# Moving the ternary weight rounding of a gated attention and feed-forward block from VectorE to GpSimd, with its readers moved to later steps

## The reference

```python
def weight_quant(w):
    scale = 1.0 / jnp.clip(jnp.mean(jnp.abs(w)), 1e-05)
    return jnp.clip(jnp.round(w * scale), -1, 1) / scale
...
h = bit_linear(x, w1)                       # 256 -> 1024, activations rounded to 8 bits, w1 ternary
h = depthwise_conv1d(h.transpose(0, 2, 1), conv_w, conv_b)
h = jax.nn.silu(h.transpose(0, 2, 1))
return bit_linear(h, w2)                    # 1024 -> 256, the same way
...
x = x + jnp.tanh(g_xattn[0]) * attention(_layernorm(x), ctx_1024, ctx_1024, Wq, Wk, Wv, Wo)   # 16 heads of 16
x = x + jnp.tanh(g_ffn[0]) * ffn(_layernorm(x), w1, conv_w, conv_b, w2)
```

## Time and profile before

| | us |
|---|---|
| median of 3 runs | 236.0 |
| lowest and highest | 234.7, 236.79 |
| span of the profiled execution | 235.2 |
| TensorE busy in it | 215.8 |
| VectorE busy | 190.4 |
| ScalarE busy | 161.9 |
| GpSimd busy | 122.2 |

### The profile page before, as it was taken

The page is one execution under the profiler, slowest core; times in us unless marked ns, Lnnn a source line. Parts: engine busy times, 40 slices in busy tenths (PEclk is TensorE's granted clock), DMA queues, the critical chain, the costliest instruction groups (busy, mean ns, idle before and its releaser), DMA issues.

```text
span 235.2 us, 6424 instructions
## 1 busy us (share of the span) xinstructions
PE 215.8 (92%) x2439; PEld 180.1 (77%) x2452; DVE 190.4 (81%) x387; ACT 161.9 (69%) x318; POOL 122.2 (52%) x229
## 2 busy tenths in 40 slices
PE   7999999997999999999999999989985699997974
PEld 7887787886878787887878878768783588886963
DVE  4163548789798999999999999999899859999671
ACT  2557768777687888989889788667933356674741
POOL 2421326364365757668677576657567224433470
PEclk9999999999999999999999999999999589999999
DMA  5982011010110101100000000000000000111111
GB/s 168 370 270 67 3 49 38 10 46 3 45 47 3 46 3 45 40 11 22 3 3 3 3 0 3 1 3 0 3 0 0 24 25 22 47 46 45 49 52 60
DMA packets 9488, 9.86 MB, mean 42 GB/s; under 512 B 1010, under 2 KB 9202, under 8 KB 9458
## 3 DMA queue, kind: packets, MB, share of 16 engines
q1 hardware_dynamic: 9458, 9.46, 12.2%
HBM read 7.36 MB, written 2.10 MB: 40 GB/s over the span
## 4 chain that ended last, share of the span: by engine, by line
PE 68%; DVE 21%; issue 5%; ACT 3%; DMA 1%; POOL 1%; SPq 0%; ACTq 0%; DVEq 0%; POOLq 0%
PE ps_score L464 10%; PE ps_proj L430 8%; PE ps_proj L509 6%; PE ps_av L487 6%; PE ps_max L474 6%; PE ps_proj L422 5%; DVE zmax L1151 5%; PE ps_proj L413 4%; PE ps_h L568 4%; PE ps_av L707 4%; DVE y L1041 4%; DVE y L1044 3%; DVE smax L987 3%; PE ps_av L497 2%; PE ps_proj L401 2%
## 5 line engine op out<-in xcount | busy, mean ns | idle before, releaser
L987 DVE TENSOR_REDUCE smax<-ps_max 128x8 f32<-128x1024 f32 x31 | 37.9, 1223 | 13.9 <-PE ps_max L474 10.7
L789 ACT ACTIVATE prob<-ps_score 128x1024 f32<-128x1024 f32 x32 | 32.7, 1023 | 17.8 <-PE ps_score L464 16.9
L464 PE MATMUL ps_score<-Qs,KT 32*128 32x128 f32 x512 | 37.1, 283 | 2.0 <-DVE smax L987 0.8
L464 PEld LDWEIGHTS ps_score<-Qs,KT 32*128 32x128 f32 x512 | 31.3, 186 | 9.3 <-issue 5.0
L474 PE MATMUL ps_max<-KT,QT 32*128 32x256 f32 x248 | 35.1, 400 | 0.0
L359 POOL TENSOR_SCALAR zq<-y,zmax 128x1024 f16<-128x1024 f32 x16 | 17.9, 1119 | 29.1 <-issue 18.1
L1151 DVE TENSOR_REDUCE zmax<-y 128x1 f32<-128x1024 f32 x16 | 19.4, 1214 | 5.3 <-ACT y L935 5.3
L336 POOL TENSOR_SCALAR xn<-xn,qa 128x256 f32<-128x256 f32 x16 | 8.1, 508 | 28.1 <-DVE qa L1027 28.1
L829 ACT ACTIVATE y<-hid,conv 128x512 f32<-128x512 f32 x24 | 18.6, 807 | 4.3 <-DVE hid L1034 3.9
L707 PE MATMUL ps_av<-w2q,zqT 128*128 128x256 f16 x128 | 17.4, 281 | 4.3 <-ACT zqT L941 2.6
L474 PEld LDWEIGHTS ps_max<-KT,QT 32*128 32x128 f32 x248 | 21.1, 184 | 0.1
(11 more groups left out here) (140 smaller groups left out, 551.9 us busy)
## 6 DMA issues: line engine op xcount, KB each, us to landing
cin<-ctxT SPq DMA_DIRECT2D x16, 128.0 KB, 2.1
xres<-x SPq DMA_DIRECT2D x16, 128.0 KB, 2.5
out<-xres SPq DMA_DIRECT2D x16, 128.0 KB, 1.7
w1f<-w1T SPq DMA_DIRECT2D x1, 1024.0 KB, 6.2
w2f<-w2T SPq DMA_DIRECT2D x1, 1024.0 KB, 8.1
wk<-wkT SPq DMA_DIRECT2D x1, 256.0 KB, 2.8
wv<-wvT SPq DMA_DIRECT2D x1, 256.0 KB, 4.4
wq<-wqT SPq DMA_DIRECT2D x1, 256.0 KB, 4.6
```

What stands on the lines that cost most here:

```text
L464: mm = pe.matmul(ps_score[:, i * 512 + j * P:i * 512 + (j + 1) * P], KT[b % 3][rows, j * P:(j + 1) * P], Qs[rows, j * P:(j + 1) * P], star ...
L789: act.activation(prob[pair][:, :], ps_score[:, :], ACT.Exp, scale=DH ** -0.5).then_inc(exp_done, 1)
L987: dve.tensor_reduce(dst, first_max(n, pair)[:, :].rearrange("p (g t e k) -> p g t e k", g=PG, t=KD, e=2), AX.X, ALU.max).then_inc(max_done, 1)
```

## The change

The 24 instructions of `ternary` leave VectorE and are issued on GpSimd instead, behind `x_mean` at the end of a step: two pieces of the first weight at the ends of steps 3 and 4, one piece of the second weight at the ends of steps 5, 6, 7 and 8. The arithmetic is regrouped: scaling and the rounding constant in one instruction, both clamps in the second, the constant taken off in the third. `weight_scale(1)` now stands right behind `quantise1` in VectorE's step 4. `SUMS_STEP` goes from 7 to 10, and with it the column sums and their copy; the two halves of `first_weights` go from ScalarE's steps 5 and 6 to steps 9 and 11.

```diff
-SUMS_STEP = SB + 3
+SUMS_STEP = SB + 6
...
+            def ternary(k, wf, wt, i, step_done, done):
+                n = KD * HID // PIECES
+                wf, wt = wf[:, k * n:(k + 1) * n], wt[:, k * n:(k + 1) * n]
+                gp.wait_ge(scale_done, i + 1)
+                gp.tensor_scalar(wf, wf, w_scale[:, i:i + 1], ROUND, ALU.mult, ALU.add).then_inc(step_done, 1)
+                gp.wait_ge(step_done, 2 * k + 1)
+                gp.tensor_scalar(wf, wf, ROUND + 1.0, ROUND - 1.0, ALU.min, ALU.max).then_inc(step_done, 1)
+                gp.wait_ge(step_done, 2 * k + 2)
+                gp.tensor_scalar(wt, wf, -ROUND, 1.0, ALU.add, ALU.mult).then_inc(done, 1)
+
...
+            first = (w1f, w1q, 0, wq1_step, w1q_done)
+            second = (w2f, w2q, 1, wq2_step, w2q_done)
+            pieces = {3: [(0, first), (1, first)], 4: [(2, first), (3, first)]}
+            pieces.update({5 + k: [(k, second)] for k in range(PIECES)})
...
                 if seq(s + 3):
                     gp.wait_ge(sh1_done, s + 3)
                     x_mean(s + 3)
+                for k, weight in pieces.get(s, ()):
+                    ternary(k, *weight)
...
             step(4, weight_sum(1, 1))
-            step(5, first_weights(0))
+            step(5)
             act.wait_ge(small_in, 16)
-            step(6, first_weights(1))
-            for s in range(SB + 3, NB - 1):
+            for s in range(SB + 2, SB + 5):
+                step(s)
+            step(SB + 5, first_weights(0))
+            step(SB + 6)
+            step(SB + 7, first_weights(1))
+            for s in range(SB + 8, NB - 1):
                 step(s)
...
-                dve.tensor_scalar(wf, wf, w_scale[:, i:i + 1], 1.0, ALU.mult, ALU.min).then_inc(step_done, 1)
...
-                dve.tensor_scalar(wf, wf, -1.0, ROUND, ALU.max, ALU.add).then_inc(step_done, 1)
...
-                dve.tensor_scalar(wt, wf, ROUND, None, ALU.subtract).then_inc(done, 1)
...
             step(2, lambda k: weight_scale(0) if k == 1 else None)
-            step(3, pieces(0, w1f, w1q, 0, wq1_step, w1q_done))
-            step(4, pieces(2, w1f, w1q, 0, wq1_step, w1q_done, scale=1))
-            step(5, pieces(0, w2f, w2q, 1, wq2_step, w2q_done))
+            step(3)
+            step(4, lambda k: weight_scale(1) if k == 1 else None)
+            step(5)
             dve.wait_ge(small_in, 16)
-            step(6, pieces(2, w2f, w2q, 1, wq2_step, w2q_done))
+            step(6)
```

More of the change, by code:

```diff
@@ L1045, in outer_taps @@
                                          y3[:, :, 0:P - 1], ALU.mult, ALU.add).then_inc(conv_done, 1)
[L1047 to L1050, removed]
-                dve.tensor_scalar(wf, wf, w_scale[:, i:i + 1], 1.0, ALU.mult, ALU.min).then_inc(step_done, 1)
-                dve.wait_ge(step_done, 2 * k + 1)
-                dve.tensor_scalar(wf, wf, -1.0, ROUND, ALU.max, ALU.add).then_inc(step_done, 1)
-                dve.wait_ge(step_done, 2 * k + 2)
-                dve.tensor_scalar(wt, wf, ROUND, None, ALU.subtract).then_inc(done, 1)
             def remainder(d):
```

## The result

The changed kernel takes 237.87 us (median of 9 runs, 236.79 to 239.24) where the kernel before takes 236.48 beside it (9 runs, 234.70 to 237.22). The ratio is 1.0068 with a 95% interval of 1.0039 to 1.0096: slower by 0.9 to 2.3 us, where I had forecast 4.4 and a range from 238.2. The sign held, the size did not. By the prediction's own measure, in which 1% tells a change from none, 0.7% even counts as the same, to which it gave 0.09. The forecast of 240.4 was added to a median of 236.0; measured beside the changed kernel, the kernel before has 236.48, so it is the difference that has to be compared.

What follows compares the result with a forecast made beforehand. The prediction took TensorE to bound the kernel; 1.8 + 1.7 + 0.1 + 0.8 = 4.4 us on a span of 235.2 gave 239.6, and 0.8 from span to median made 240.4 us, range 238.2 to 244.0.

Steps and rivals of the forecast that it cites:

- What bounds the kernel: Whole kernel: TensorE, busy 215.8 of 235.2 us; the added work must fit two loops, through GpSimd and up to ScalarE's xnT.
- What goes: Before step 5, TensorE's 1.06 us wait for w_mean is the only gain; moving the sums to step 10 gives nil.
- The price of a piece: On GpSimd: 0.69, 0.62 and 0.62 us for three instructions plus gaps, 2.2 us a piece and 4.4 for two.
- Rival 1: GpSimd's pieces are dearer than interpolated, for instance through min and max: 243.4 or 245.4 us; chance 0.12.
- Steps 4 to 6: Two pieces a GpSimd turn exceed the 2.9 us of room, delaying quantise1 and project_q: 1.8 us behind by step 6.
- Steps 6 to 10: One piece a GpSimd turn: turns from step 7 too long by 0.43 us, plus 0.3 for tap clashes; 1.7 us.
- rival 2: Steps 7 to 9: GpSimd keeps up, pieces and taps interleaving without loss, turn 9.15 us; 239.4 us; chance 0.22.
- ScalarE: Half of first_weights ahead of the xnT copy costs 0.8 us in step 11 and adds 0.1 in step 9.
- The sum: Whole kernel: 1.8 + 1.7 + 0.1 + 0.8 = 4.4 us on a span of 235.2, giving 239.6.

Runs made afterwards that it cites:

- the order alone: The kernel before, with weight_scale(1) ahead of instead of behind the last ternary piece of VectorE's step 4; ratio 0.9951 (0.9933 to 0.9970), 1.2 us faster.

## Why the prediction was right in sign and wrong in size

**What bounds the kernel** held: TensorE's steps, and the two loops through GpSimd and ScalarE. One sentence fell: that the wait for `w_mean` is all that VectorE's ternary work costs. It was all that shows. Another 0.94 us lay under the sums in step 7.

**What goes** had two errors that cancel in the changed kernel. I put the move of the sums at nil; alone it costs 0.94. In the changed kernel steps 7 and 10 give -1.04 and +1.05, since the pieces have left VectorE in the same edit.

**The price of a piece** held to 0.02 us an instruction, the clamps included. Rival 1 falls.

**Steps 4 to 6** is the step that failed: forecast +1.8, measured -0.79 + 0.18 + 0.89 = +0.28. The mechanism was right (`quantise1` waits, `w_mean` behind it, then `xn` and `xnT`), the term was mis-sized. I took `norm2` at 2.27 us and the start of the loop at 49.25 from a trace in which VectorE's ternary instructions ran at the same time, and the change removes just those. Undisturbed it is 1.90, `x_mean` ends 0.25 earlier (`round1` to `x_mean` takes 3.11 us and not 3.36, since VectorE's piece no longer runs beside it), and I counted the gaps around the pieces 0.3 too high. A turn is 10.16 and not 10.77; two turns and the earlier start make 0.6 x 2 + 0.25 = 1.5 of the 1.5 us that are missing. The runs with one piece a turn and with the pieces behind `norm2` show the loop itself: each brings steps 4 to 6 back to TensorE's pace.

**Steps 6 to 10** is the other term that failed, in size again: forecast +1.7, plus 0.1 in step 9; measured +0.04 and +0.23 in steps 7 and 8, +0.28 in step 9 once ScalarE's copy is out of the way, 0.55 in all. The turn is 9.9 us (75.31 to 85.20 and to 95.11). I had put it at 10.06 and 0.3 for clashes; the terms of the 10.06 add up to 10.14, so the sum was also 0.08 short. Against 10.44 two terms are too high. The 0.3 us of clashes came to nothing net: I left `norm2` at its disturbed 3.27 us behind a piece that pushes it off part of the taps, and 3.27 with my 2.3 for the piece gives the 5.57 that step 7 has. And from `norm2`'s end to `round1` it is 1.21 us (83.99 to 85.20) and not 0.1 + 1.27 + 0.09 = 1.46. So a turn is 0.26 us too long for a step and not 0.73. Rival 2's mechanism, a turn of 9.15 without loss, did not come true either: `norm2` got shorter (2.69 us for 3.18 over the taps), but the piece longer (2.8 us for 2.1 in step 7, from its first start to its last end). The time came out nearer to rival 2, which puts this stretch at nothing.

**ScalarE** held: 0.8 forecast in step 11, 0.73 measured, and 0.74 in step 9, which the larger of two lates decides.

**The sum**: 4.4 forecast, 1.99 by the steps, 1.6 (0.9 to 2.3) by the timed runs. Between executions of the same clock the difference lies around the 1.99 of the steps. At a mean clock of 0.989 to 0.993 the changed kernel's spans have a mean of 236.0 us (7 executions) and those of the kernel before 234.2 (59, from the runs of the experiments): +1.7. At 0.983 to 0.984 it is 237.3 (1) against 235.1 (24), and at 1.0 235.0 (1) against 232.4 (4). One of nine executions of the changed kernel fell to the lower of these values and 24 of 87 of the kernel before. With so few executions that can be chance: that the timed runs show less than the steps may come from the clock in the last part, but whether the change itself favours the clock stays open.

## What to carry to other kernels

Take a duration for a sum from a row in which the instruction's neighbours are those that it will have after the change; the same `norm2` took 2.27 us beside the work that was to go and 1.90 without it. Work that is moved to an idle engine costs by its place in that engine's loop and not by its length: six instructions cost 1.4 us behind `x_mean` and nothing behind `norm2`, where the gap was just long enough to hold them; a single piece behind `norm2` in step 7, where taps run beside it, cost 0.4 us. And before moving the thing that bounds a step, look at which engine was full under it: the sums covered 0.9 us of VectorE.

## What the runs showed of the hardware that I had not expected

GpSimd takes the pair of min and max with two constants over 512 columns in 0.61 us, the same as adding and multiplying. Where taps and pieces overlap, both lengthen by parts of each other (1.11 and 0.91 us for 0.69 and 0.61; 1.06 for 0.75), and in step 7 the blocked time of the turn stayed within 0.2 us of what it was without the piece. VectorE's ternary instructions (0.43 to 0.59 us each) lengthen GpSimd's instructions of a single column: `rstd` from 0.57 to 0.81 us, `x_mean` from 0.24 to 0.45. TensorE's granted clock fell to its lower level between 182 and 190 us in nine of the twelve traces. In the two in which most of the fillers ahead of that stretch are gone it fell at 176 to 180. In one, all pieces behind `norm2`, it never fell, though TensorE was busy for only 0.67 us between 180 and 184, no more than the 0.68 of the run with the order alone, where it fell: the busy time of that stretch alone does not decide it. Where it stayed high, the part from step 15 on took 78.7 us; in the other traces it took 79.9 to 81.4, a scatter of up to 2.8 us, larger than the effect under study. The lengths of the steps that an edit leaves alone agree to 0.01 us between runs, and tell more than the spans do.
